# Second channel half of two conditioned norms: scale and shift on ScalarE, one operation per sequence

## The reference

```python
def norm(x, t, gw, gb, bw, bb):
    g = (t @ gw.T + gb)[:, None, :]
    b = (t @ bw.T + bb)[:, None, :]
    inv_rms = rsqrt(mean(x * x, axis=-1, keepdims=True) + 1e-6)
    return g * x * inv_rms + b

x1 = x + attention(norm(x, t, g1...), Wq, Wk, Wv, Wo)        # 16 heads of 16
y  = x1 + swiglu(norm(x1, t, g2...), gate_w, hid_w, out_w)   # hidden 1024
return x + y
```

## Time and profile before

| | |
|---|---|
| runs | 1078.95, 1081.28, 1076.1 us; median 1078.95 |
| profiled execution, its own time | 1077.67 us |
| its span, first to last instruction | 1075.9 us |
| mean granted TensorE clock | 0.992 |
| busy share TensorE / VectorE / ScalarE / GpSimd | 96% / 63% / 39% / 32% |

### The profile page before, as it was taken

One profiled execution on the slowest core, in us unless ns is written; L12 is line 12 of the kernel. 1 busy time (PEld: TensorE's weight loads), 2 busy tenths in 40 slices (PEclk: granted clock), 3 DMA queues, 4 the chain that ended last, 5 costly groups with the idle time before them and its releaser, 6 DMA issues.

```text
span 1075.9 us, 22083 instructions
## 1 busy us (share of the span) xinstructions
PE 1032.2 (96%) x8240; PEld 919.7 (85%) x8240; DVE 673.7 (63%) x1306; ACT 423.5 (39%) x903; POOL 339.5 (32%) x284
## 2 busy tenths in 40 slices
PE   6879999999999999999999999999999999999987
PEld 5768889889888988988888888988988898898876
DVE  4645766566666656766666676657666665666543
ACT  3433343444334343343434434344433434334232
POOL 4313233232333223233232323323233323324142
PEclk9979999999999999999999999999999999999999
DMA  4100000010100001010010100001010000100000
GB/s 169 41 1 21 2 24 18 1 39 0 39 0 19 19 0 39 0 39 0 0 39 0 39 0 25 14 0 39 0 39 0 19 19 0 39 0 21 1 21 19
DMA packets 18968, 21.67 MB, mean 20 GB/s; under 512 B 640, under 2 KB 18240, under 8 KB 18816
## 3 DMA queue, kind: packets, MB, share of 16 engines
q1 hardware_dynamic: 18720, 21.24, 5.9%
q10 hardware_dynamic: 224, 0.10, 0.0%
HBM read 12.95 MB, written 8.39 MB: 20 GB/s over the span
## 4 chain that ended last, share of the span: by engine, by line
PE 67%; issue 23%; POOL 5%; ACT 2%; DVE 2%; DMA 0%; POOLq 0%; ACTq 0%; DVEq 0%; SPq 0%
PE ps L824 8%; PE ps L737 6%; PE ps L809 6%; PE ps L739 6%; PE ps L738 5%; PE ps L817 5%; PE ps L832 4%; PE ps L842 4%; PE ps L845 4%; PE ps L835 4%; PE ps L843 4%; PE ps L833 4%; POOL h_lo L247 4%; PE ps L744 1%; PE ps L853 1%
## 5 line engine op out<-in xcount | busy, mean ns | idle before, releaser
L247 POOL TENSOR_TENSOR h_lo<-shared,h_hi 128x512 fp32r<-128x512 f32 x128 | 164.7, 1286 | 360.5 <-ACT h_hi L371 313.3
L577 DVE SCALAR_TENSOR_TENSOR shared<-shared,ps 128x512 f32<-128x512 f32 x128 | 87.8, 686 | 128.1 <-ACT shared L366 127.6
L737 PE MATMUL ps<-out_w_hi,h_hi 128*128 128x256 f32 x512 | 154.1, 301 | 9.5 <-POOL h_lo L247 9.5
L366 ACT ACTIVATE shared<-ps 128x512 f32<-128x512 f32 x128 | 76.4, 597 | 194.1 <-PE ps L835 125.2
L739 PE MATMUL ps<-out_w_hi,h_lo 128*128 128x256 f32 x512 | 144.4, 282 | 0.0
L738 PE MATMUL ps<-out_w_lo,h_hi 128*128 128x256 f32 x512 | 143.7, 281 | 0.0
L824 PEld LDWEIGHTS ps<-values,probsT 128*128 128x128 f32 x1024 | 129.8, 192 | 13.2 <-ACT probsT L376 8.0
L376 ACT ACTIVATE probsT<-ps 128x512 f32<-128x512 f32 x128 | 74.7, 597 | 163.8 <-PE ps L817 163.8
L824 PE MATMUL ps<-values,probsT 128*128 128x66 f32 x1024 | 130.8, 271 | 4.0 <-ACT probsT L376 4.0
L371 ACT CAST h_hi<-shared 128x512 fp32r<-128x512 f32 x128 | 78.9, 616 | 99.7 <-DVE shared L584 99.7
L563 DVE TENSOR_REDUCE row_max<-ps 128x8 f32<-128x512 f32 x128 | 87.8, 686 | 37.7 <-PE ps L809 36.7
(11 more groups left out here) (101 smaller groups left out, 2150.9 us busy)
## 6 DMA issues: line engine op xcount, KB each, us to landing
x_in<-in_x SPq DMA_DIRECT2D x16, 512.0 KB, 3.4
out<-result SPq DMA_DIRECT2D x15, 512.0 KB, 2.9
shared<-in_attT SPq DMA_DIRECT2D x1, 1024.0 KB, 7.0
shared<-in_gateT SPq DMA_DIRECT2D x1, 1024.0 KB, 8.9
shared<-in_hidT SPq DMA_DIRECT2D x1, 1024.0 KB, 4.8
shared<-in_outT SPq DMA_DIRECT2D x1, 1024.0 KB, 5.5
out<-result SPq DMA_DIRECT2D x2, 256.0 KB, 2.2
result<-in_modT SPq DMA_DIRECT2D x1, 256.0 KB, 4.7
```

The lines of the kernel that those rows point to most:

```text
L247: nc.gpsimd.tensor_tensor(h_lo[:, j % 2, :], h[:, :], h_hi[:, j % 2, :].bitcast(F32), ALU.subtract).then_inc(h_lo_done, 1)
L737: nc.tensor.matmul(dst, a_hi, b_hi, start=first, stop=False, skip_group_check=skip)
```

## The change

ScalarE takes the second half (c = 1) of both norms: eight activations, one for each sequence (64 columns), which read the transposed tile from PSUM and write gain x value + shift, with gain and shift as pointers to one number per partition. VectorE keeps the first half. The low part of norm 2's second half moves from GpSimd to VectorE, between the row maximum and the shift of pair 0. In the queues, `second_norm1` stands behind exp 6 and ahead of `high_norm1`; `second_norm2` stands ahead of `high_norm2`. TensorE's `scores` waits for `gained2` (now the first half alone) and `xn2_second`, and its chunk 6 for `gained1` and `xn1_second`. The core of the diff (declarations of semaphores, and the same edits for the first tile, left out):

```diff
+            def low_norm2(u):                      # GpSimd
+                pool.wait_ge(xn2_hi_done, CH * u + 1)
+                wait(pool, hid_mm, CHUNKS * u)
+                nc.gpsimd.tensor_tensor(xn2_lo[:, 0, :], xn2[:, 0, :], xn2_hi[:, 0, :].bitcast(F32),
+                                        ALU.subtract).then_inc(xn2_lo_first, 1)
...
+            def second_norm(u, m, src, transposed, read, xn, done):     # ScalarE
+                act.wait_ge(transposed, CH * u + CH)
+                wait(act, read[0], read[1])
+                for b in range(SEQS):
+                    tok = slice(b * L, (b + 1) * L)
+                    last = nc.scalar.activation(xn[:, 1, tok], src[:, tok], ACT.Identity,
+                                                bias=mod[:, m + 1, 1, bass.ds(u * SEQS + b, 1)],
+                                                scale=mod[:, m, 1, bass.ds(u * SEQS + b, 1)])
+                last.then_inc(done, 1)
+
+            def second_norm1(u, bank):
+                second_norm(u, 0, ps[:, bank, :], xT1_done, (xn1_lo_done, CH * u), xn1, xn1_second)
+
+            def second_norm2(u):
+                second_norm(u, 2, ps[:, PAIR + 3, :], xT2_done, (xn2_lo_second, u), xn2, xn2_second)
...
             def high_norm1(u, c):
-                act.wait_ge(xn1_done, CH * u + c + 1)
+                act.wait_ge((xn1_first, xn1_second)[c], u + 1)
...
                 if ahead:
+                    second_norm1(t + 1, HIDDEN)
                     high_norm1(t + 1, 0)
                     high_norm1(t + 1, 1)
...
                 if attend:
+                    second_norm2(t)
                     high_norm2(t, 0)
                     high_norm2(t, 1)
...
+            def low_norm2(u):                      # VectorE
+                dve.wait_ge(xn2_hi_done, CH * u + 2)
+                wait(dve, hid_mm, CHUNKS * u)
+                nc.vector.tensor_tensor(xn2_lo[:, 1, :], xn2[:, 1, :], xn2_hi[:, 1, :].bitcast(F32),
+                                        ALU.subtract).then_inc(xn2_lo_second, 1)
...
                 if attend:
-                    maxima_and_shift(t, 0)
+                    row_maxima(t, 0)
+                if mlp:
+                    low_norm2(t - 1)
+                if attend:
+                    shift(t, 0)
                     maxima_and_shift(t, 1)
...
                 if ahead:
-                    for c in range(CH):
-                        gain(t + 1, c, 0, GATE + c, xT1_done, xn1, xn1_lo_done, gained1)
-                    for c in range(CH):
-                        add_shift(t + 1, c, 1, xn1, gained1, xn1_done)
+                    first_norm1(t + 1, GATE)
...
-                    for c in range(CH):
-                        gain(t, c, 2, PAIR + 2 + c, xT2_done, xn2, xn2_lo_done, gained2)
-                    for c in range(CH):
-                        add_shift(t, c, 3, xn2, gained2, xn2_done)
+                    first_norm2(t)
...
-                    wait(pe, gained2, CH * t)
+                    wait(pe, gained2, t)
+                    wait(pe, xn2_second, t)
...
-                        pe.wait_ge(gained1, CH * t + 2 * CH)
+                        pe.wait_ge(gained1, t + 2)
+                        pe.wait_ge(xn1_second, t + 2)
```

More of the change, by code:

```diff
@@ L134, in conditioned_block @@
         ms1_done, mse1_done, inv1_done, scaled1 = map(sem, ["ms1_done", "mse1_done", "inv1_done", "scaled1"])
-        xT1_done, gained1, xn1_done, xn1_hi_done, xn1_lo_done = map(
-            sem, ["xT1_done", "gained1", "xn1_done", "xn1_hi_done", "xn1_lo_done"])
+        xT1_done, gained1, xn1_first, xn1_second, xn1_hi_done, xn1_lo_done = map(
+            sem, ["xT1_done", "gained1", "xn1_first", "xn1_second", "xn1_hi_done", "xn1_lo_done"])
         q_mm, q_act_done, q_dve_done, k_mm, k_act_done, k_dve_done, v_mm, v_even, v_odd = map(
@@ L143, in conditioned_block @@
         ms2_done, mse2_done, inv2_done, scaled2 = map(sem, ["ms2_done", "mse2_done", "inv2_done", "scaled2"])
-        xT2_done, gained2, xn2_done, xn2_hi_done, xn2_lo_done = map(
-            sem, ["xT2_done", "gained2", "xn2_done", "xn2_hi_done", "xn2_lo_done"])
+        xT2_done, gained2, xn2_first, xn2_second, xn2_hi_done, xn2_lo_first, xn2_lo_second = map(
+            sem, ["xT2_done", "gained2", "xn2_first", "xn2_second", "xn2_hi_done", "xn2_lo_first", "xn2_lo_second"])
         gate_mm, hid_mm, tanh_done, silu_done, h_done, h_hi_done, h_lo_done, down_mm, result_done = map(
@@ L229, in inverse_rms @@
                 nc.gpsimd.tensor_tensor(inv[:, :], mse[:, :], minus_half[:, :], ALU.pow).then_inc(inv_done, 1)
[L231 to L236, removed]
-            def low_norm1(u, c):
-                low_norm(u, c, xn1, xn1_hi, xn1_lo, xn1_hi_done, xn1_lo_done, v_mm, 2 * u)
-            def low_norm2(u, c):
-                low_norm(u, c, xn2, xn2_hi, xn2_lo, xn2_hi_done, xn2_lo_done, hid_mm, CHUNKS * u)
+            def low_norm1(u, c):
+                pool.wait_ge(xn1_hi_done, CH * u + c + 1)
+                wait(pool, v_mm, 2 * u)
+                nc.gpsimd.tensor_tensor(xn1_lo[:, c, :], xn1[:, c, :], xn1_hi[:, c, :].bitcast(F32),
+                                        ALU.subtract).then_inc(xn1_lo_done, 1)
+            def low_norm2(u):
[3 more added lines that the diff above has]
+                                        ALU.subtract).then_inc(xn2_lo_first, 1)
             def low_hidden(u, j):
@@ L298, in iteration @@
                 if attend:
-                    low_norm2(t, 0)
-                    low_norm2(t, 1)
+                    low_norm2(t)
             over_tiles(pool, iteration)
@@ L334, in high_norm2 @@
             def high_norm2(u, c):
-                act.wait_ge(xn2_done, CH * u + c + 1)
+                act.wait_ge((xn2_first, xn2_second)[c], u + 1)
                 wait(act, hid_mm, CHUNKS * u)
@@ L383, in _ @@
             act.wait_ge(consts_in, 16)
+            act.wait_ge(mod_done, 2 * CH)
+            second_norm1(0, PAIR + 1)
             for c in range(CH):
@@ L503, in of_sequences, with gain, add_shift, first_norm1 @@
                 return mod[:, m, c, bass.ds(u * SEQS, SEQS)].unsqueeze(2).to_broadcast([P, SEQS, L])
[L505 to L509, removed]
+            def gain(u, m, bank, transposed, xn, read, gained):
+                dve.wait_ge(transposed, CH * u + 1)
+                wait(dve, read[0], read[1])
+                nc.vector.tensor_tensor(xn[:, 0, :].rearrange("p (b q) -> p b q", q=L),
                                         ps[:, bank, :].rearrange("p (b q) -> p b q", q=L),
[L511 to L516, removed]
+                                        of_sequences(m, 0, u), ALU.mult).then_inc(gained, 1)
+            def add_shift(u, m, xn, gained, done):
+                dve.wait_ge(gained, u + 1)
+                dst = xn[:, 0, :].rearrange("p (b q) -> p b q", q=L)
+                nc.vector.tensor_tensor(dst, dst, of_sequences(m, 0, u), ALU.add).then_inc(done, 1)
+            def first_norm1(u, bank):
+                gain(u, 0, bank, xT1_done, xn1, (xn1_lo_done, CH * u), gained1)
+                add_shift(u, 1, xn1, gained1, xn1_first)
+            def first_norm2(u):
+                gain(u, 2, PAIR + 2, xT2_done, xn2, (xn2_lo_first, u), gained2)
+                add_shift(u, 3, xn2, gained2, xn2_first)
+            def low_norm2(u):
[3 more added lines that the diff above has]
+                                        ALU.subtract).then_inc(xn2_lo_second, 1)
             def second_keys(u):
@@ L609, in _ @@
             scale_rows(0, x_in, inv1, inv1_done, x_scaled1, xT1_done, scaled1)
-            for c in range(CH):
-                gain(0, c, 0, PAIR + c, xT1_done, xn1, xn1_lo_done, gained1)
-                add_shift(0, c, 1, xn1, gained1, xn1_done)
+            first_norm1(0, PAIR)
             for c in range(CH):
@@ L861, in first_chunk_low @@
                     for i in range(CH):
-                        pe.wait_ge(xn2_lo_done, CH * u + i + 1)
+                        pe.wait_ge((xn2_lo_first, xn2_lo_second)[i], u + 1)
                         last = nc.tensor.matmul(ps[:, bank, :], hi[:, i, 0:P], xn2_lo[:, i, :], start=False,
```

## The result

The changed kernel takes **1122.66 us** (median of 4 runs, 1120.81 to 1123.77) where the kernel before takes 1077.74 (median of its 4 runs by then). The ratio is 1.0399, 95% interval 1.038 to 1.0419: slower by 45 us, where the forecast was 1120 us and 41 us more (range 1105 to 1136). The profiled execution took 1123.77 us with a span of 1121.9, which is 46.0 us more than the profiled span before.

What follows compares the result with a forecast made beforehand. The prediction took the loop as a TensorE stream with under 1 us of waiting per tile. 26.6 + 9.2 + 2.8 + 2.2 = 40.8 us on 1077.67, plus 1.28 from profiled execution to median, gave 1120 us, range 1105 to 1136.

Steps and rivals of the forecast that it cites:

- Price of an activation: ScalarE in both norms: 0.40 us for 64 columns with two pointers, spaced 0.30, so eight take 2.50 us.
- The two bounds: Limits for eight activations: 0.8 us from the shortest ScalarE operation, 4.0 us from 256 columns with a second pointer added.
- Norm 1: At chunk 6's gate matmul: TensorE idles 1.9 us for activations queued behind exp 6, 14 times, 26.6 us.
- Norm 2 and the shift of pair 0: Scores 0.66 us late, 9.2 us in 14 tiles; pair 0's shift, behind VectorE's low piece, 0.2 us each, 2.8 us.
- What was costed at nothing: After the eight in the loop: norm 1's casts and GpSimd low halves, tanh 6, pair 1's transposes; no further stall.
- Ends: Outside the loop: 1.8 us between tiles 0 and 1, some 0.4 at the last tile, 2.2 us together.
- Within 0.5 us of before, I count nothing: Tile 0: project_k's low halves come within 0.5 us of before, pair 7's shift wait shortens; counted as nothing.
- rival (1): Clock falls at each loop stall, 2.5 us a tile, 1155 us; chance 0.09 shared with the case of long activations.
- Relief of VectorE: Rival: less VectorE work pays, but only in tile 0's 3.30 us wait, 3 us in all, 1076 us; chance 0.02.

Runs made afterwards that it cites:

- ahead_of_exp6: The changed kernel with second_norm1 moved ahead of exp 6 in ScalarE's queue, nothing else: 1100.32 us, ratio 1.0192 to the kernel before.
- one_activation: The changed kernel with one activation of 512 columns in place of each eight of 64, both pointers kept: 1084.64 us, ratio 1.0053 to the kernel before.
- norm2_only: The changed kernel with norm 1's edits undone, so only norm 2's second half goes to ScalarE: 1094.29 us, ratio 1.0126 to the kernel before.
- no_pointers: The changed kernel with its eight activations as plain copies, without scale and bias pointers: 1089.13 us, ratio 1.0102 to the kernel before.

## Why the prediction was right, point by point

- **Price of an activation:** 0.40 us, 0.30 apart, eight in 2.50 us. Measured 0.414 to 0.422, 0.29 to 0.30 apart ((2.48 - 0.414)/7), eight in 2.47 and 2.48. The two bounds, 0.8 and 4.0 us, were far off; for the eight, the estimate put together from a slope, a base and a pointer's price was right to 1%, for one of them to 5%. The Trainium skill's formula (ScalarE: Activation LUTs, What ACT_TABLE_LOAD costs) makes an estimate of 425 ns, which the row supports, and of 332 for the spacing, where the trace has 295.
- **Norm 1:** The forecast was 1.9 us in 14 tiles, 26.6 us. Measured 26.8 by the marks. That it is the queue behind exp 6 is shown by `ahead_of_exp6` (22 us less), and that it is the eight fixed costs by `one_activation`.
- **Norm 2 and the shift of pair 0:** The forecast was 9.2 + 2.8 = 12.0 us. Measured 11.7, 0.70 a tile for the scores (0.66 forecast) and 0.15 for the moved low half (0.2 forecast).
- **What was costed at nothing:** In the loop GpSimd's low halves of norm 1, tanh 6 and pair 1's transposes made no wait: the table of waits after has no row for them.
- **Ends:** 2.2 us. This is the term that was mis-sized: 7.5 in the profiled pair. Some 2.4 lie at the start, where the order of VectorE and GpSimd differs from profile to profile; `norm2_only`, whose start is that of the kernel before, shows 2.7, so they need not come of the change. The other 5 are tile 0 (1.6 where I counted nothing), the step from tile 0 to 1 (3.2 where I had 1.8) and the end (0.4 as forecast). The stretches between the marks tell waiting and clock apart, tile 0 and then the step to tile 1, first in the kernel before and then in the changed one (columns as above); the last two rows are the changed kernel's first stall of the tile above and its project_k in tile 0:

```profile
42.40:73.49 31.09, 26.42 (x217) 23.24 (x215) 18.30 (x42) 10.41 (x22) 8.26 (x6) 0.89 0.01 2
73.49:106.42 32.93, 28.71 (x209) 25.36 (x210) 16.98 (x33) 12.70 (x28) 9.92 (x9) 0.84 0.05 17
...
44.84:77.49 32.65, 26.63 (x217) 23.03 (x215) 17.20 (x40) 12.48 (x30) 8.24 (x6) 0.90 0.01 2
77.49:113.59 36.10, 30.14 (x209) 26.46 (x210) 16.31 (x32) 14.98 (x36) 8.71 (x7) 0.81 0.05 15
...
592.00:597.00 5.00, 3.32 (x27) 3.06 (x27) 3.08 (x7) 3.68 (x11) 0.13 (x1) 1.00 0.00 0
...
61.30 0.79 PE L766 MATMUL ps<-xn_hi,att_w_hi 128*128 128x512 f32 x1 [2.40 <-POOL xn_lo L234]
```

  In tile 0 TensorE is busy as long as before and idles 1.35 us more: the wait for pair 7's shift is 1.1 us shorter, but project_k now waits 2.40 us for GpSimd's xn_lo. "Within 0.5 us of before, I count nothing" was wrong there; with the eight ahead of exp 6 and norm 2 as before (`norm1_ahead_only`) that wait doesn't appear. In the step to tile 1 the wait at the scores grew from 0.9 to 2.7 us, the 1.8 that I had, and the same 209 matmuls keep TensorE busy 1.43 us longer at a mean clock of 0.81 instead of 0.84: rival (1) on a small scale, which I had not put into this term. In the loop the clock stayed at 1.00 through the stalls of 1.7 us, so rival (1) as a whole is refuted.
- **What was luck:** The change cost 44.9 us between the medians and I had 40.8. The time came out closer, 2.7 us off, since the median from which I started was 1.2 us above that of all four runs.
- **Relief of VectorE:** It brought no gain in the loop, as the earlier trace rows said, and 1.1 us less of one wait in tile 0. VectorE is 24 us less busy, not some 30: gains, shifts and the low piece went from 82.6 to 56.2 us (two in a row overlap and count once), and the first scalings took 2.2 us more.

## What to carry to other kernels

A transfer of work off the critical engine is priced by when its last piece ends and by what stands before it in the new engine's queue, not by busy shares. ScalarE, 39% busy, stood idle for 1.3 of the 2.6 us between the transposes and gate 6, but at the head of its queue was exp 6, whose input wasn't there yet. Moving the new work ahead of it won back 1.56 of the 1.91 us. Splitting one operation of 512 columns into eight of 64 multiplies the fixed part by eight, and the pointers for scale and bias go with more than half of the eight's 2.48 us; where a path has 1.5 us of room, that decides. Look for the gain in the bounding engine's own table of waits: one of 0.5 us, 14 times, was worth 8 to 9 us for one subtraction moved from GpSimd to VectorE.

## What the runs showed of the hardware that I had not expected

- Four VectorE scalings of 128x256 fp32 from SBUF to SBUF take 1.14 us alone and up to 5.4 us beside GpSimd's 128x1024 subtractions. They are held, not slowed: one or two of them take 2.43 us and the others 0.35. An fp32 addition of two SBUF tensors is held too (2.34 us for 0.69); a multiplication with an operand in PSUM is not (0.69 beside the same work). The Trainium skill says this of the pair of SBUF ports that the two engines share (SBUF — State Buffer, SBUF: two separate sides: an exclusive lock for the whole instruction). The profiles differ by some 2 to 4 us through it, by whichever of the two starts first near 10 us; how much of the spread between unprofiled executions it makes is not shown.
- Addresses of pointers that are worked out at run time cost ScalarE 0.15 to 0.22 us between a wait and the first activation. In the iteration ahead of the loop, where they are constants, the eight of tile 1's norm 2 start 0.04 us after the transposes end; in the loop they start 0.18 to 0.19 after (619.14 against 617.92 + 1.04); and with no pointers (`no_pointers`) 0.03 in the loop as well. The first pair is the changed kernel's tile 1, the second `no_pointers` in the loop:

```profile
151.93 1.03 PE L781 MATMUL ps<-consts_sb,shared 128*128 128x128 f32 x8
153.00 2.48 ACT L333 ACTIVATE shared<-ps,mod 128x64 f32<-128x64 f32 x8 [0.92 <-PE ps L781]
...
592.47 1.04 PE L779 MATMUL ps<-consts_sb,shared 128*128 128x128 f32 x8
593.54 1.04 ACT L333 ACTIVATE shared<-ps 128x64 f32<-128x64 f32 x8 [0.92 <-PE ps L779]
```

  At norm 1 with the eight ahead of exp 6 it is 0.26 in the loop against 0.04 in the iteration before it, and the marks follow: norm 1 costs 0.35 us a tile in the loop there and 0.16 ahead of it, and norm 2 in the changed kernel 0.85 and 0.67. Behind exp 6 the changed kernel's norm 1 shows no such difference (1.91 us ahead of the loop, 1.93 in the tile above), so there it seems to be hidden while exp 6 runs. The forecast had 0.14 for this start everywhere.
- Short activations overlap more than long ones: 64 columns without pointers take 254 to 264 ns and are spaced 0.11 us ((1.03 - 0.26)/7), an overlap of some 0.15, where operations of 512 columns have 0.10.
